# Ring of x1 by half tiles, mid turned a step later, first normalise in two halves and added transposes in a linear cross attention with a LoRA mixture

## The reference, cut to what matters

```python
def xattn(q, k, v):                  # (B, C, N), dh = C/8 = 64 channels per head
    qh = softmax(q per head, over the dh channels)
    kh = softmax(k per head, over N)
    kvs = einsum('bnhd,bnhe->bhde', kh, vh)
    return einsum('bnhd,bhde->bnhe', qh, kvs)
def ffn(x, router_w, A, B):          # 4 experts, rank 16, top 2
    gates = softmax(top-2 of x @ router_w.T)
    mid = einsum('tf,erf->ter', x, A)
    return einsum('te,teo->to', gates, einsum('ter,eor->teo', mid, B) * 4)
x = x + xattn(layernorm(x), ctx, ctx)
x = x + ffn(layernorm(x), router_w, A, B)
```

## Time and profile before

| | before |
|---|---|
| median of 3 runs | 434.94 us (434.35 to 435.05) |
| profiled execution | 434.23 us |
| its span | 432.4 us |
| TensorE busy (matmul / weight load) | 401.3 / 368.6 us |
| VectorE, ScalarE, GpSimd busy | 340.5, 339.8, 359.5 us |
| moved | 137.57 MB |

### The profile page before, as it was taken

How to read it: one execution, slowest core, us unless ns; L and a number is a source line. 1 busy time by engine, 2 the same in 40 slices (tenths; PEclk the granted TensorE clock), 3 DMA queues, 4 the chain that set the end, 5 groups by cost and what they waited for, 6 DMA issues and landing times.

```text
span 432.4 us, 16682 instructions
## 1 busy us (share of the span) xinstructions
PE 401.3 (93%) x6858; PEld 368.6 (85%) x6858; DVE 340.5 (79%) x887; ACT 339.8 (79%) x469; POOL 359.5 (83%) x343
## 2 busy tenths in 40 slices
PE   6478988999999999999999999999999999999974
PEld 6368877898999989998999989998999989999864
DVE  2846678989888897889888898889878998666764
ACT  1589979995999779995999779995999679994410
POOL 0959989998999989898999989898999989994510
PEclk9669999999999999999999999999999999999988
DMA  8999987799999999999999999999999998656248
GB/s 288 416 413 408 304 274 255 246 300 361 331 345 339 360 353 354 365 353 348 332 351 347 349 357 363 361 348 343 342 343 353 338 352 264 204 186 196 104 177 304
DMA packets 37898, 137.57 MB, mean 318 GB/s; under 512 B 4160, under 2 KB 4288, under 8 KB 37696
## 3 DMA queue, kind: packets, MB, share of 16 engines
q1 hardware_dynamic: 37824, 136.52, 88.1%
HBM read 102.95 MB, written 33.55 MB: 316 GB/s over the span
## 4 chain that ended last, share of the span: by engine, by line
PE 59%; DVE 22%; issue 7%; DMA 4%; ACT 3%; POOL 2%; SPq 2%; DVEq 0%; POOLq 0%; ACTq 0%
PE num_ps L441 23%; PE kv_ps L425 10%; PE raw_ps L457 10%; DVE attnT L760 6%; PE kv_ps L471 5%; DMA ctx_sb<-in_ctxt_dram 4%; DVE bn_parts L698 4%; DVE max_n L682 3%; PE delta_ps L508 3%; PE delta_ps L509 3%; DVE y_sb L777 2%; DVE rden L753 2%; POOL y_sb L352 1%; PE delta_ps L403 1%; PE kv_ps L410 1%
## 5 line engine op out<-in xcount | busy, mean ns | idle before, releaser
L352 POOL TENSOR_TENSOR y_sb<-attnT,y_sb 128x512 f32<-128x512 f32 x127 | 162.6, 1281 | 31.4 <-DVE attnT L760 30.7
L340 POOL TENSOR_TENSOR ek_sb<-ctx_sb,kmax_row 128x512 f32<-128x512 f32 x128 | 167.9, 1314 | 13.0 <-ACT kmax_row L561 13.0
L441 PE MATMUL num_ps<-kv_sb,x_sb 128*128 128x130 f32 x1024 | 144.9, 285 | 7.3 <-DVE attnT L760 3.5
L441 PEld LDWEIGHTS num_ps<-kv_sb,x_sb 128*128 128x128 f32 x1024 | 126.6, 193 | 17.2 <-DVE attnT L760 11.4
L760 DVE TENSOR_TENSOR attnT<-num_ps,rden 128x512 f32<-128x512 f32 x128 | 88.4, 690 | 2.5 <-DVE rden L753 0.4
L682 DVE TENSOR_REDUCE max_n<-ctx_sb 128x64 f32<-128x1024 f32 x64 | 76.9, 1205 | 12.3 <-DMA ctx_sb<-in_ctxt_dram 12.3
L425 PE MATMUL kv_ps<-ctx_sb,ek_sb 128*64 128x65 f32 x2048 | 79.1, 230 | 1.8 <-ACT ek_sb L583 1.8
L590 ACT ACTIVATE x_sb<-x_sb,nbias,rstd 128x1024 f32<-128x1024 f32 x64 | 78.9, 1232 | 0.0
L425 PEld LDWEIGHTS kv_ps<-ctx_sb,ek_sb 128*64 128x64 f32 x2048 | 69.7, 140 | 10.6 <-issue 2.6
L777 DVE TENSOR_TENSOR y_sb<-delta_ps,y_sb 128x1024 f32<-128x1024 f32 x60 | 73.3, 1222 | 4.5 <-PE delta_ps L509 4.2
L457 PE MATMUL raw_ps<-w_sb,y_sb 128*64 128x69 f32 x2048 | 74.1, 224 | 0.9 <-POOL y_sb L352 0.8
(11 more groups left out here) (72 smaller groups left out, 407.8 us busy)
## 6 DMA issues: line engine op xcount, KB each, us to landing
ctx_sb<-in_ctxt_dram SPq DMA_DIRECT2D x64, 520.0 KB, 7.9
x_sb<-in_x_dram SPq DMA_DIRECT2D x64, 512.0 KB, 6.5
y_sb<-in_xt_dram SPq DMA_DIRECT2D x64, 512.0 KB, 6.9
out_dram<-y_sb SPq DMA_DIRECT2D x63, 512.0 KB, 8.5
y_sb<-in_bt_dram SPq DMA_DIRECT2D x1, 1024.0 KB, 17.7
w_sb<-in_wt_dram SPq DMA_DIRECT2D x1, 552.0 KB, 12.4
out_dram<-y_sb SPq DMA_DIRECT2D x2, 256.0 KB, 3.8
cst<-in_consts_dram SPq DMA_DIRECT2D x1, 145.0 KB, 2.3
```

The source lines that it names most:

```text
L340: pool.tensor_tensor(ek_sb[:, t % 2, chunks(g), :].rearrange("p (a b) c -> p a b c", b=2), ctx_sb[:, t % 4, 2 * g:2 * g + 2, 1:P + 1, :].r ...
L352: pool.tensor_tensor(y, attnT[:, g, :], y, ALU.add).then_inc(x1_made, 1)
L441: mm = pe.matmul(num_ps[:, j // 2, at:at + 2 * (DH + 1)], x_sb[:, t % 4, c * P:(c + 1) * P], kv_sb[:, t % 2, :], start=True, stop=True, sk ...
```

## The change

Five edits. (1) `normalise(t, 0)` writes its two halves by two instructions, the first of which releases the first two chunks of numerator (t, 1). (2) `turn_mid`, `mid_high` and `mid_low` come one step (two quarters) later, deltas and their additions and the stores too; `turn_mid` now stands ahead of the second numerator of its step; `bn_part` is divided two and two between the steps. (3) The ring: each half tile has its own store semaphore, the second half of the turned x is loaded at q = 4t + 4 instead of 4t + 2, and the loads no longer wait for `raw_done`. (4) The last two pairs are stored by quarters. (5) `keep_busy` puts transposes with an unused result between TensorE's work at the start and in the tail.

```diff
-        out_stored = [sem(f"out_stored{i}") for i in range(8)]
+        out_stored = [[sem(f"out_stored{i}_{k}") for k in range(2)] for i in range(8)]
@@ delta_at, adds_until
-            p, i = divmod(q - 22, 8)
+            p, i = divmod(q - 24, 8)
...
-            return max(0, min((q - 22) // 2, 4 * NP))
+            return max(0, min((q - 24) // 2, 4 * NP))
@@ sync
-            for q in range(0, 4 * NT + 28, STEP):
+            for q in range(0, 4 * NT + 30, STEP):
                 last = q + STEP - 1
-                p, r = divmod(q - 26, 8)
-                if 0 <= p < NP - 1:
+                p, r = divmod(q - 28, 8)
+                if 0 <= p < NP - 2:
...
-                t, r = divmod(q, 4)
-                if 2 <= t < NT:
-                    after(sp, raw_done, quarters_done(q, 8))
-                    if t == 7:
-                        sp.wait_ge(b_lo_made, 4)
-                    if t >= 8:
-                        sp.wait_ge(out_stored[t % 8], 16 * PIECES * (t // 8))
-                    load_y(t, r // STEP)
+                for k in range(PIECES):
+                    t, r = divmod(q - 4 * k, 4)
+                    if r == 0 and 2 <= t < NT:
+                        if t == 7:
+                            sp.wait_ge(b_lo_made, 4)
+                        if t >= 8:
+                            sp.wait_ge(out_stored[t % 8][k], 16 * (t // 8))
+                        load_y(t, k)
...
-            for i in range(3):
-                sp.wait_ge(out_made, 4 * (NP - 1) + i + 1)
-                store_last(i)
+            for n in range(4 * (NP - 2), 4 * NP - 1):
+                sp.wait_ge(out_made, n + 1)
+                store_pair(n // 4, n % 4)
@@ tensor, numerator
-                after(pe, attn_made, 4 * t + g)
+                if g == 1:
+                    pe.wait_ge(attn_half, t + 1)
+                else:
+                    after(pe, attn_made, 4 * t + g)
                 for j in range(CH):
+                    if g == 1 and j == 2:
+                        pe.wait_ge(attn_made, 4 * t + 1)
@@ tensor, loop
+            def keep_busy(to, n):
+                for _ in range(n):
+                    pe.transpose(to, ident, ident)
...
                 spread_kmax(tile_in(q, -4))
+                keep_busy(unused, {-4: 30, 4: 4, 6: 8}.get(q, 0))
+                turn_mid(pair_in(q, 22))
                 numerator(*tile_at(q + 1, 6))
-                turn_mid(pair_in(q, 20))
                 for k in range(2):
                     kv(*tile_at(q + k, 0))
+                keep_busy(unused, 8 if q == 0 else 0)
...
             p = NP - 1
+            turn_mid(p - 1)
+            for i in range(6, 8):
+                delta(p - 2, i)
...
+            keep_busy(unused, 14)
+            for i in range(4, 6):
+                delta(p - 1, i)
+            keep_busy(unused, 3)
             turn_mid(p)
+            keep_busy(unused, 5)
@@ scalar: step q % 4 == 2
                     square_x1(T - 2, 1)
+                    mid_high(pair_in(q, 22))
@@ vector, normalise
+                to = attnT[:, g, :].rearrange("p (b k d) -> p b k d", b=2, d=DH)
+                if g > 0:
+                    dve.tensor_tensor(to, heads[:, :, :, 0:DH], rden[:].unsqueeze(3).to_broadcast([P, 2, CH, DH]),
+                                      ALU.mult).then_inc(attn_made, 1)
+                else:
+                    for b, made in enumerate((attn_half, attn_made)):
+                        dve.tensor_tensor(to[:, b], heads[:, b, :, 0:DH],
+                                          rden[:, b, :].unsqueeze(2).to_broadcast([P, CH, DH]),
+                                          ALU.mult).then_inc(made, 1)
@@ vector, loop and tail
-                mid_low(c)
-                for g in range(1) if q % 4 == 0 else range(1, 4):
+                mid_low(pair_in(q, 22))
+                for g in range(2) if q % 4 == 0 else range(2, 4):
...
             p = NP - 1
+            add_delta(p - 2, 6)
+            mid_low(p - 1)
```

More of the change, by code:

```diff
@@ L168, in xattn_lora_moe_kernel @@
         attn_made = sem("attn_made")
+        attn_half = sem("attn_half")
         out_made = sem("out_made")
@@ L265, in store, with store_pair @@
                 sp.dma_start(out[t, :, c, :].rearrange("p j c -> p (j c)"),
-                             y_sb[:, t % 8, c, :].rearrange("p j c -> p (j c)")).then_inc(out_stored[t % 8], 16)
-            def store_last(i):
+                             y_sb[:, t % 8, c, :].rearrange("p j c -> p (j c)")).then_inc(out_stored[t % 8][k], 16)
+            def store_pair(p, i):
                 c = slice(4 * i, 4 * i + 4)
-                sp.dma_start(out[NT - 2:NT, :, c, :].rearrange("t p j c -> p t (j c)"),
-                             y_sb[:, pair_slots(NP - 1), c, :].rearrange("p t j c -> p t (j c)")
+                sp.dma_start(out[2 * p:2 * p + 2, :, c, :].rearrange("t p j c -> p t (j c)"),
+                             y_sb[:, pair_slots(p), c, :].rearrange("p t j c -> p t (j c)")
                              ).then_inc(last_stored, 16)
@@ L327, in _ @@
             for k in range(8):
-                uses = len(range(k, NT - 2, 8))
-                sp.wait_ge(out_stored[k], 16 * PIECES * uses)
-            sp.wait_ge(last_stored, 16 * 5)
+                uses = len(range(k, NT - 4, 8))
+                for piece in out_stored[k]:
+                    sp.wait_ge(piece, 16 * uses)
+            sp.wait_ge(last_stored, 16 * 9)
         @block.gpsimd
@@ L503, in delta @@
                         after(pe, out_made, n)
-                        after(pe, kmax_made, min((8 * p + i + 22) // 4 + 2, NT))
+                        after(pe, kmax_made, min((8 * p + i + 24) // 4 + 2, NT))
                 for k in range(2):
@@ L514, in sum_w @@
                 pe.matmul(raw_ps[1][:, 0, 0:ER + E], ones, w_fold[:], start=True, stop=True).then_inc(w_summed, 1)
+            def keep_busy(to, n):
+                for _ in range(n):
+                    pe.transpose(to, ident, ident)
+            unused = raw_ps[0][:, 0, 0:P]
             pe.wait_ge(cst_landed, 16)
-            for _ in range(40):
-                pe.transpose(raw_ps[0][:, 0, 0:P], ident, ident)
+            keep_busy(unused, 40)
             for q in range(FIRST, 4 * NT + 6, 2):
@@ L545, in _ @@
             sum_squares(NT - 1)
-            for i in range(2, 6):
+            unused = kv_ps[1][:, 0:P]
+            for i in range(2, 4):
                 delta(p - 1, i)
+            keep_busy(unused, 14)
+            for i in range(4, 6):
+                delta(p - 1, i)
+            keep_busy(unused, 3)
             turn_mid(p)
+            keep_busy(unused, 5)
             for i in range(6, 8):
@@ L656, in _ @@
                     queries(T - 1, 0)
-                    mid_high(pair_in(q, 20))
                     sum_x(T + 1)
@@ L759, in normalise @@
                 after(dve, x1_made, 4 * (t - 1) + g + 1)
-                dve.tensor_tensor(attnT[:, g, :].rearrange("p (b k d) -> p b k d", b=2, d=DH),
-                                  heads[:, :, :, 0:DH], rden[:].unsqueeze(3).to_broadcast([P, 2, CH, DH]),
-                                  ALU.mult).then_inc(attn_made, 1)
+                to = attnT[:, g, :].rearrange("p (b k d) -> p b k d", b=2, d=DH)
[7 more added lines that the diff above has]
+                                          ALU.mult).then_inc(made, 1)
             def add_x_last():
```

## The result

The changed kernel takes 497.28 us (median of 6 runs, 495.45 to 501.04) beside 434.64 us (434.01 to 435.10) of the kernel before: a ratio of 1.145, 95% interval 1.141 to 1.149. It is 62.6 us slower. The forecast was slower by 19, 454 us in a range up to 474: the direction is right and the size far too small. The profiled execution has a span of 493.9 us, 61.5 more than before.

A forecast was written before the change was run, and what follows sets the result against it. TensorE, 93% busy, and the transfers were taken as nearly full. A loop through y1's late landing adds 19.9 us and the tail takes 1.0 from 434.23; with 0.7 for the median, 454 us, range 436 to 474.

The forecast's parts named there:

- What decides: Ring by halves: y1, issued later behind load_x, lands too late for add_x(t, 0); 19.9 us more over 27 tiles.
- the loop: SP's x load, y1's landing, add_x, shift, root1, bias, normalise, numerator, next x load; period at least L + 5.17 us.
- L: Time from x's issue to y1's landing, third in its burst: 7.3 us before stores, 7.8 after; binds from 6.95.
- low end: L 7.05 us everywhere, from the nearest burst of three before the first store; 436 us total.
- high end: L 9.05 us once there are stores: x alone 6.1 plus 2.95 to the third landing; 483 us total.
- the sum: 5 tiles of 12.45 and 22 of 12.95 us against about 327.3 us: 19.9 more, tail -1.0, giving 454 us.
- The links: Loop after y1's landing: add_x, shift, root1 3.06 us, handover 0.05, bias, normalise and numerator 2.06; 5.17 us taken.
- Split normalise: normalise g=0 in halves shrinks TensorE's gap before numerator g=1 from 0.33 us per tile; 8 us counted.
- Mid a step later: turn_mid's two transposes move into TensorE's gap every second tile; zero beyond the gap counted, bounds -1 and +3 us.
- Start: Extra transposes keep TensorE's clock up, but VectorE waits for a ctx_sb transfer; zero, bounds -1 and +0.5 us.
- Tail: Extra transposes may recover VectorE's waits for deltas at reduced clock; -1 us, bounds -1.7 and +1.
- the harder loop: Rival: stores crowd the burst as they crowd x, L over 8.5 us, 470 us and up; chance 0.15.

The follow-up runs named there:

- the loads ahead of x: The changed kernel with both y loads of an iteration issued ahead of load_x and its wait for the numerator: 426.99 us, ratio 0.983.

## Why the prediction was right or wrong

**What decides: right.** The mechanism was forecast link by link, with the tiles it strikes: 27 of 27. Moving the load alone brings the whole loss, opening the loop at either of two places removes it, and shortening L shortens the period. The 5.17 us for the links other than the landing were measured as 5.13 in the turn shown; the mean is 5.4.

**L, the landing of the second half: the step that failed.** Forecast 7.3 and 7.8 us, low end 7.05 and high end 9.05; measured 9.0 in the mean, 7.2 to 10.5 from turn to turn. What was mis-sized is the way from x's landing to that of the third transfer: 2.95 us, read from one burst, against 4.5 in the mean. The queue ahead of x was indeed shorter, by more than was thought, and x landed in 4.4 us where 6.1 stood in the high end; but the prediction carried that over to the two transfers behind x, and they do not profit from it: L is 8.2 even with no store in the queue at all. That the high end met the mean is luck, since its 6.1 was too long and its 2.95 too short by about as much. Two smaller things come with it. The burst of the earlier trace rows came out of a stretch without stores, and the stores are worth 0.8 us of L. And the issues cost more: the chain gives SP 6% of 493.9 us, 1.1 us per turn where the sum had 0.8, with single y issues of 1.51 us, and the landing 41%, 7.5 us per turn from its own issue where the sum had 7.0. The sum's 7.0 was hardly above the median of the earlier trace rows, 6.9 us, which is of single y loads and not of the third in a burst.

**The links: mostly right, one missing.** The first turns are longer than L + 5.17: from x at 47.61 to the next at 62.67 are 15.06 us with L at 7.44. There, before q = 22, `project` stands ahead of the second numerator on TensorE, and so add_x(t, 1) is in the loop as well:

```profile
55.05 1.27 POOL y_sb L354
56.32 1.25 POOL ek_sb L342
57.57 0.51 POOL rstd L361
58.08 1.24 POOL y_sb L354
...
59.37 0.71 PE raw_ps L464 x16
...
60.91 1.75 PE num_ps L448 x8
```

The numerator at its end takes 1.75 us instead of 1.18. The window of that turn, then its last part (length, PE, PEld, DVE, ACT, POOL, clock, DMA share, GB/s):

```profile
47.60:62.60 15.00, 11.77 (x198) 10.36 (x198) 8.81 (x20) 10.28 (x13) 11.56 (x11) 0.91 0.63 213
60.00:62.60 2.60, 2.60 (x17) 2.37 (x13) 0.00 (x0) 1.66 (x3) 2.60 (x3) 0.51 0.00 0
```

TensorE now stands idle up to 3.9 us at a time, and behind such a wait its granted clock is about half, 1.2 GHz, so that the mean is 0.91 here and 0.955 over the span, where the steady windows had 1.00. The prediction left both out.

**The sum.** 26 periods from 47.61 to 424.35 take 14.49 us each where 12.85 was forecast: (14.49 - 12.85) x 27 = 44 us, and the miss is 43.3. Of the 1.64 us per tile, 9.07 - 7.70 = 1.37 is L (9.07 is its mean over the 26 turns) and the rest the links. The period lies outside the 12.4 to 13.5 us that were named as its sign. There is a slip in the sum as well: 7.3 + 5.17 and 7.8 + 5.17 are 12.47 and 12.97, not 12.45 and 12.95, which makes 0.5 us in all.

**Split normalise: right in mechanism and size.** 8 us forecast, 7.4 and 6.9 measured, and rightly given as not won while the loop is closed.

**Mid a step later: right.** Taken at zero; without the split the kernel with the later mid, the later stores and the added transposes is 0.3% faster than before.

**Start: right**, zero. **Tail: not shown.** -1 us was forecast; from the last x issue to the end of the span it is 69.5 us in the changed kernel and 69.6 before. With the loads ahead of x it is 68.3, with and without the transposes, and 68.5 in the kernel before with the split alone.

**The rule of the Trainium skill.** By the Trainium skill (DMA: Bandwidth & Descriptors, Anatomy of one DMA), which fits one DMA issued by GpSimd where SP issues all of them here, the third transfer would have landed an estimated 5.6 us after the first was issued, and nothing would have been lost. The runs show 7.2 at the least and 9.0 in the mean, and 8.2 where hardly anything is under way ahead; the measurement decides.

**The range.** It gave the harder loop 0.15. With bounds of 7.05 and 9.05 for L the sum went up to 483, and the range was cut at 474. Even the uncut one would have missed by 14 us, since the bounds of L were put together from single rows.

**Open.** Why the two transfers behind x take 4.0 us even without any stores, where the earlier trace rows have 2.95, is not settled; the DMA engines are busy in that time. It was not tried to change the size of the pieces or the engine that issues them.

## What to carry to other kernels

Before a load is moved later, look for what its issue now stands behind in the queue: when that is itself released by work that needs the load, the slack is spent once and then a loop is closed, and the whole landing time is paid in every turn. The cheapest remedy is to let each consumer wait for the piece that it reads; here one semaphore per half is worth 66 us. And the landing time in such a loop is not to be read from one burst: the second and third transfer of it took 4.5 us in the mean where one burst showed 2.95, and a shorter queue ahead of the burst helped its first transfer alone.

## What was not expected of the hardware

Transfers of 512 KB issued back to back behind each other land at very unequal distance: add_x could start on the same second half 7.2 to 10.5 us after x was issued, in a steady loop. And the order in the burst counts for more than a transfer's own time at the full rate, an estimated 1.3 us for 512 KB at the 413 GB/s of the start: exchanging two loads moved L by 1.8 us and the kernel by 51. A queue that has run dry is no disadvantage for the first transfer behind it, which landed in 4.1 us against 5.9 in the kernel before.
